# A second attention whose logits come from H times (W a), ELU moved between heads, and norms that read a sum of four chunks

## What is computed

```python
def gat_layer(x, W, a_src, a_dst, bias, src, dst, heads, out_c, concat):
    h = (x @ W).reshape(n, heads, out_c)
    al_s = jnp.einsum('nhc,hc->nh', h, a_src)      # source logit of each node
    al_d = jnp.einsum('nhc,hc->nh', h, a_dst)      # target logit of each node
    e = jax.nn.leaky_relu(al_s[src] + al_d[dst], 0.2)
    m = jax.ops.segment_max(e, dst, num_segments=n)
    ex = jnp.exp(e - m[dst])
    z = jax.ops.segment_sum(ex, dst, num_segments=n)
    alpha = ex / (z[dst] + 1e-16)
    msg = h[src] * alpha[:, :, None]
    out = jax.ops.segment_sum(msg, dst, num_segments=n)
    ...
# layer 1: second layer on elu(first layer): gat_layer(h, W2, a_src2, a_dst2, b2, ..., 1, 768, False)
```

## Time and profile before

| what | value |
|---|---|
| median of 3 runs | 3227.3 us (3222.09 to 3234.06) |
| profiled execution: its own time | 3223.88 us |
| its span, first to last instruction | 3222.1 us |
| mean granted TensorE clock | 0.970 |
| PE busy | 3017.0 us, 94% |
| DVE, ACT, POOL busy | 1723.8, 742.5, 1435.7 us |

### The profile page before, as it was taken

The page is one execution under the profiler, slowest core; times in us unless marked ns, Lnnn a source line. Parts: engine busy times, 40 slices in busy tenths (PEclk is TensorE's granted clock), DMA queues, the critical chain, the costliest instruction groups (busy, mean ns, idle before and its releaser), DMA issues.

```text
span 3222.1 us, 38156 instructions
## 1 busy us (share of the span) xinstructions
PE 3017.0 (94%) x13743; PEld 2340.4 (73%) x13753; DVE 1723.8 (53%) x2816; ACT 742.5 (23%) x1288; POOL 1435.7 (45%) x1007
## 2 busy tenths in 40 slices
PE   8999898999999996998998889899999998999988
PEld 3467576878888884776877358578888886878855
DVE  7734699575545537745785645533333336743132
ACT  1043211242223312102235221211111112212122
POOL 2022377624454442464541044456666664545610
PEclk9999999999999998998999899999999999999999
DMA  2011257311222221222210142123323332222313
GB/s 84 15 44 45 98 178 219 94 39 60 73 69 74 73 65 59 71 89 63 81 53 30 50 132 64 59 76 98 93 88 98 97 98 64 79 68 75 102 36 137
DMA packets 91282, 256.96 MB, mean 80 GB/s; under 512 B 10343, under 2 KB 10983, under 8 KB 90868
## 3 DMA queue, kind: packets, MB, share of 16 engines
q1 hardware_dynamic: 79488, 217.09, 22.1%
q10 hardware_dynamic: 11668, 38.19, 3.5%
HBM read 253.67 MB, written 1.57 MB: 79 GB/s over the span
## 4 chain that ended last, share of the span: by engine, by line
PE 84%; DVE 10%; issue 4%; ACT 2%; DMA 0%; ACTq 0%; DVEq 0%
PE ps L437 23%; PE ps L441 22%; PE ps L442 22%; PE ps L921 3%; DVE aux L2130 2%; PE ps L549 1%; PE ps L543 1%; PE ps L802 1%; PE ps L813 1%; PE ps L795 1%; PE ps L787 1%; DVE hot L2583 1%; DVE row L1938 1%; PE ps L622 1%; PE ps L1008 1%
## 5 line engine op out<-in xcount | busy, mean ns | idle before, releaser
L372 POOL TENSOR_SCALAR w_hi<-raw 128x768 fp32r<-128x768 f32 x498 | 469.3, 942 | 1607.5 <-PE ps L437 1418.3
L375 POOL TENSOR_TENSOR w_lo<-raw,w_hi 128x768 fp32r<-128x768 f32 x498 | 974.9, 1958 | 41.5
L437 PE MATMUL ps<-A_hi,w_hi 128*128 128x512 f32 x924 | 364.5, 394 | 2.2 <-DVE sel_now L2411 1.5
L441 PE MATMUL ps<-A_lo,w_hi 128*128 128x512 f32 x924 | 360.7, 390 | 0.0
L442 PE MATMUL ps<-A_hi,w_lo 128*128 128x512 f32 x924 | 360.2, 390 | 0.0
L437 PE MATMUL ps<-H_hi,w_hi 128*128 128x512 f32 x804 | 319.3, 397 | 22.3 <-issue 11.6
L441 PE MATMUL ps<-H_lo,w_hi 128*128 128x512 f32 x804 | 316.4, 394 | 0.0
L442 PE MATMUL ps<-H_hi,w_lo 128*128 128x512 f32 x804 | 315.9, 393 | 0.0
L437 PE MATMUL ps<-B_hi,w_hi 128*128 128x512 f32 x576 | 234.4, 407 | 13.6 <-DVE B_lo L1916 7.4
L441 PE MATMUL ps<-B_lo,w_hi 128*128 128x512 f32 x576 | 226.6, 393 | 0.0
L442 PE MATMUL ps<-B_hi,w_lo 128*128 128x512 f32 x576 | 226.5, 393 | 0.0
(11 more groups left out here) (510 smaller groups left out, 5632.3 us busy)
## 6 DMA issues: line engine op xcount, KB each, us to landing
raw<-stream_dram SPq DMA_DIRECT2D x552, 384.0 KB, 3.0
w_ring<-w_dram ACTq DMA_DIRECT2D x43, 384.0 KB, 3.8
u_rows<-rows_dram ACTq DMA_DIRECT2D x8, 768.0 KB, 6.0
rows<-rows_dram ACTq DMA_DIRECT2D x7, 768.0 KB, 4.0
w_last<-w_dram ACTq DMA_DIRECT2D x9, 384.0 KB, 3.6
x<-x_dram ACTq DMA_DIRECT2D x1, 1536.0 KB, 8.9
out_dram<-x ACTq DMA_DIRECT2D x1, 1536.0 KB, 5.1
orf<-orf_dram ACTq DMA_DIRECT2D x6, 192.0 KB, 3.1
```

The costliest lines, as they stand in the source:

```text
L372: pool.tensor_scalar(w_hi[:, b // 3, b % 3], raw[:, b // 3, b % 3], 1.0, 1.0, ALU.mult, ALU.mult)\
L375: pool.tensor_tensor(w_lo[:, b // 3, b % 3], raw[:, b // 3, b % 3], w_hi[:, b // 3, b % 3], ALU.subtract)\
L437: mm = pe.matmul(o, wh, xh, start=first, stop=False, skip_group_check=True)
L441: pe.matmul(o, wh, xl, start=False, stop=False, skip_group_check=True)
```

## The change

1. Layer 1's second attention. While layer 0's experts run, ScalarE loads the two attention rows and W2's six row blocks, and VectorE makes `u2` = W2 a for both rows (`out_vectors`: 12 multiply-and-sum instructions of 768 and two small ones). In `turn_n`'s first group TensorE adds, behind each chunk, three products of `u2` (2 columns) with the chunk of H: a 2x512 row of logits. VectorE copies it, TensorE turns its target part into columns and broadcasts its source part inside the second group, and `gat_rows(1)` runs in the middle of that group. `terms`, `source_row` and `gat_rows(0)` are gone. The copies of the product are made straight from PSUM, and the last two tiles' copies come behind the edge weights.
2. The ELU of chunks 0, 1 and 2 goes between the scalings of heads 4 to 7; chunks 3, 4 and 5 follow. The turned chunks use banks 4 and 5.
3. Six norms read `x[0]+x[1]+x[2]+x[3]` that VectorE has added into `scr[:, 5]` (three additions between the chunks of `gat_sum` or `add_t`), then chunks 4 and 5: three products in place of six. The additions run in every iteration of the loops `experts2` (8) and `mlp3` (4).

```diff
-            def norm(since=None):
+            def norm(since=None, summed=False):
                 use(6)
-                for j in range(KC):
+                if summed:
+                    pe.wait_ge(bank_free["dve"][4], S.seen.get(bank_free["dve"][4].name, 0) + 1)
+                    pe.matmul(ps[:, 6], ones[:, :], scr[:, 5], start=True, stop=False, skip_group_check=True)
+                for j in range(4 if summed else 0, KC):
...
+                def turned(chunks):
+                    pe.wait_ge(act_to_pe, S.due(act_to_pe))
+                    for j in chunks:
+                        b = 4 + j % 2
+                        use(b)
+                        for m in range(NT):
+                            mm = pe.transpose(ps[:, b, m * P:m * P + P], acc_n[:, m, j * P:j * P + P], ident[:, :])
+                        done(mm, b, "act")
...
+                    if h >= 5:
+                        turned(((0, 1), (2,), (3,))[h - 5])
-                unpend()
-                pe.wait_ge(act_to_pe, S.due(act_to_pe))
-                transposes(lambda m, j: acc_n[:, m, j * P:j * P + P], "act")
-                turn_n(H, "act", since=chunks_due())
-                gat_rows(0)
-                gat_rows(1)
+                turned((4,))
+                turned((5,))
+
+                def out_logits(k):
+                    if k == 0:
+                        pe.wait_ge(u2_split, 1)
+                        use(6)
+                    mm = mm3(ps[0:2, 6], u2_hi[:, k], u2_lo[:, k], H[0][:, k], H[1][:, k], k == 0, k == KC - 1)
+                    if k == KC - 1:
+                        done(mm, 6, "dve")
+
+                def out_rows(m, k):
+                    if (m, k) == (0, 2):
+                        pe.wait_ge(dve_to_pe, S.due(dve_to_pe))
+                        use(7)
+                        for n in range(NT):
+                            mm = pe.transpose(ps[:, 7, n * 2:n * 2 + 2], row[0:2, n * P:n * P + P], ident[0:2, 0:2])
+                        done(mm, 7, "dve")
+                        use(6)
+                        done(pe.matmul(ps[:, 6], ident[0:2, 0:1].to_broadcast([2, P]), row[0:2, :], start=True, stop=True), 6, "dve")
+                    if (m, k) == (1, KC - 1):
+                        pe.wait_ge(dve_to_pe, S.due(dve_to_pe))
+
+                def out_targets(g, m):
+                    if (g, m) == (1, 1):
+                        gat_rows(1)
+
+                turn_n(H, "act", mid=out_targets, since=chunks_due(), last=False, freed_by="dve", per_chunk=out_logits,
+                       inside=out_rows)
                 gat_den()
-                graph_t("dve")
+                graph_t("dve", second=True)
...
+                load_rows(ROW_L1B)
+                for k in range(KC):
+                    act.dma_start(gat_w1(k), t["w1"][GAT_W1 + KC + k]).then_inc(u2_in, 16)
...
+                gat_scaled(4)
+                elu_parts(0)
+                elu_parts(1)
+                gat_scaled(5)
+                mark(act_to_pe)
+                elu_parts(2)
+                gat_scaled(6)
+                mark(act_to_pe)
+                gat_scaled(7)
+                mark(act_to_pe)
+                for j in range(3):
+                    elu_high(j)
+                elu_parts(3)
+                elu_parts(4)
+                elu_high(3)
+                elu_parts(5)
+                elu_high(4)
+                elu_high(5)
...
+                nodes_of(0, range(NT))
+                nodes_of(1, range(2))
                 edge_weights()
+                nodes_of(1, range(2, NT))
...
+            def sum_of_x(j):
+
+                if 2 <= j < 5:
+                    S.step(dve.tensor_tensor(scr[:, 5], x[:, 0] if j == 2 else scr[:, 5], x[:, j - 1], ALU.add))
...
                 for j in range(KC):
+                    sum_of_x(j)
                     dve.wait_ge(tile_for["dve"], S.due(tile_for["dve"]))
-                    S.step(dve.tensor_tensor(scr[:, j], ps[:, j], row[:, :], ALU.mult))
+                    S.step(dve.tensor_tensor(scr[:, j % 4], ps[:, j], row[:, :], ALU.mult))
...
+            def out_vectors():
+
+                dve.wait_ge(rows_in, S.due(rows_in, 16))
+                dve.wait_ge(u2_in, KC * 16)
+                for k in range(KC):
+                    for r in range(2):
+                        ins = dve.tensor_tensor_reduce(flat[:, r * D:r * D + D], gat_w1(k), rows[:, r], 1.0, 0.0, ALU.mult, ALU.add,
+                                                       u2_all[:, k, r:r + 1])
+                    S.step(ins)
...
-                experts("experts0", 2, 10.0, True, lambda n: gat_vectors(range(3, KC)) if n == 1 else None)
+                experts("experts0", 2, 10.0, True, lambda n: gat_vectors(range(3, KC)) if n == 1 else out_vectors() if n == 3 else None)
...
+                gat_inverse(5)
+                elu_merged(0)
+                elu_merged(1)
+                gat_inverse(6)
+                elu_merged(2)
+                gat_inverse(7)
+                for j in range(3):
+                    elu_low(j)
...
+                dve.wait_ge(tile_for["dve"], S.due(tile_for["dve"]))
+                freed(dve.tensor_copy(row[0:2, :], ps[0:2, 6]), 6)
+                mark(dve_to_pe)
+                nodes_of(0, range(NT))
+                mark(dve_to_pe)
+                dve.wait_ge(tile_for["dve"], S.due(tile_for["dve"]))
+                freed(dve.tensor_copy(nv[:, 0:2, :], ps[:, 7, 0:8].rearrange("p (m r) -> p r m", r=2)), 7)
                 target_rows()
+                nodes_of(1, range(2))
                 edge_weights()
+                nodes_of(1, range(2, NT))
+                mark(dve_to_pe)
```

More of the change, by code:

```diff
@@ L485, in turn_t, with turn_n @@
                             after(3 * g + j)
-            def turn_n(X, reader, mid=None, since=None, last=True, freed_by=None):
+            def turn_n(X, reader, mid=None, since=None, last=True, freed_by=None, per_chunk=None, inside=None):
                 def tile_done(mm, b):
@@ L517, in turn_n @@
                                        k == 0, k == KC - 1)
+                            if inside:
+                                inside(m, k)
                         tile_done(mm3_, b)
@@ L521, in turn_n, with graph_t @@
                     blocks_used(3, last and g == 1)
-            def graph_t(reader, halves=False):
+            def graph_t(reader, halves=False, second=False):
                 hn = [B[h][:, :, :].rearrange("p k n -> p (k n)").rearrange("p (m d) -> p m d", m=NT) for h in range(2)]
                 for j in range(KC):
-                    if halves and j % 3 == 0:
+                    if halves and j % 3 == 0 or second and j == 3:
                         pe.wait_ge(dve_to_pe, S.due(dve_to_pe))
@@ L542, in norm @@
                         pe.wait_ge(bank_free["dve"][j], S.seen.get(bank_free["dve"][j].name, 0) + 1)
-                    mm = pe.matmul(ps[:, 6], ones[:, :], norm_src[0][:, j], start=j == 0, stop=j == KC - 1,
-                                   skip_group_check=True)
+                    mm = pe.matmul(ps[:, 6], ones[:, :], norm_src[0][:, j], start=j == 0 and not summed,
+                                   stop=j == KC - 1, skip_group_check=True)
                 done(mm, 6, "dve")
@@ L556, in norm_twice @@
             def norm_twice():
-                norm()
+                norm(summed=True)
                 return chunks_due()
@@ L1014, in part, with norm_of @@
                 return p in parts
-            def norm_of(src, since=None):
+            def norm_of(src, since=None, summed=False):
                 norm_src[0] = src
-                norm(since)
+                norm(since, summed)
             ran = lambda p: p in parts
@@ L1754, in _, with elu_parts, elu_high @@
                 mark(act_to_pe)
+                merged = [S.due(dve_to_act) for j in range(KC)]
+                def elu_parts(j):
+                    q, b = 2 * (j % 2), 4 + j % 2
+                    if j >= 2:
+                        act.wait_ge(dve_to_act, merged[j - 2])
+                    act.wait_ge(tile_for["act"], S.due(tile_for["act"]))
+                    act.activation(aux[:, q], ps[:, b], ACT.Exp, bias=col("L1_gnn_b1", j))
+                    freed(act.activation(aux[:, q + 1], ps[:, b], ACT.Relu, bias=col("L1_gnn_b1", j)), b)
+                    mark(act_to_dve)
+                def elu_high(j):
+                    act.wait_ge(dve_to_act, merged[j])
+                    act.activation(H[0][:, j], scr[:, j], ACT.Identity, bias=-1.0).then_inc(act_to_dve, 1)
                 for h in range(1, 3):
@@ L1757, in _, with nodes_of @@
                     gat_exps(h + 5)
[L1758 to L1759 removed]
                 mark(act_to_pe)
[L1761 to L1764 removed]
+                gat_scaled(3)
+                mark(act_to_pe)
[8 more added lines that the diff above has]
+                gat_scaled(7)
+                mark(act_to_pe)
+                for j in range(3):
[6 more added lines that the diff above has]
```

(17 more changed lines are left out.)

67 lines of the change are left out of this document (43 added, 24 removed).

## The result

The changed kernel takes 3197.7 us in the median of four runs (3194.0 to 3199.4), the kernel before 3228.6 beside it (3222.1 to 3234.1). The ratio is 0.9904, with a 95% interval of 0.9892 to 0.9917. That is 30.9 us less, where 32.3 were summed and 3195 was forecast. The spans of the profiled executions differ by less, 3222.1 against 3195.2 us: the profiled execution of before lies 4.8 us under its median, that of after only 0.7 us under its own.

What follows compares the result with a forecast made beforehand. TensorE, busy 94% of the span, was taken as the bound. Norms 15.4 plus gnn1's end 16.9 made 32.3 us off 3223.9, 3191.6; with 3.4 us to the median, 3195 us, range 3187 to 3209 at more than 8 in 10.

Steps and rivals of the forecast that it cites:

- Norms: Six norms each lose three chunks on TensorE, 3 x 0.857 = 2.57 us a norm, 15.4 us in all.
- The additions cost nothing: VectorE's three additions per norm, 0.65 to 2.05 us each, lie before waits for TensorE's tiles and are hidden.
- ELU and the start of turn_n: With ELU of early chunks between head scalings in gnn1, turn_n starts at 1733.5 in place of 1737.19.
- T: End of turn_n's group 0 with 18 logit products added, forecast at 1753.0 with 5.9 us at low clock.
- The rows of logits: In turn_n's second group: no wait at the row, 0.3 us before the broadcasts, last low half of edge weights at T+19.4.
- graph_t: Layer 1's graph_t starts at T+20.15 = 1773.1 in place of 1789.32, 16.2 us sooner.
- the 0.7 us extra for a full clock at its start: graph_t's first products run at full instead of low clock, saving 0.7 us more, together 16.9 us.
- Beside the experts: out_vectors' 12 products end by 1457, before TensorE needs bank 0 about 1460: no cost; at 2.4 us each, 9 us stall.
- Rival B: Middle of turn_n becomes a chain of waits and the clock falls; gnn1 gives 6 us, time 3206; chance 0.13.
- C: One of the two parts, norms or gnn1's end, gives nothing: 3210 or 3211 us; chance 0.10.
- D: Additions in the experts2 and mlp3 loops are not hidden: 2.3 us each, 83 us, 3278 us; chance 0.04.
- E: The rest, such as a stall beside the experts that eats most of the gain, no change; chance 0.03.

Runs made afterwards that it cites:

- norms_only: Kernel before with only the cheaper norms of part 3, gnn1's code left as before: 3213.9 us, ratio 0.9957 to the kernel before.
- chunk5_bank7: Changed kernel with the last ELU chunk turned into bank 7, not waiting for bank 5: 3194.6 us, 3.1 us under the changed kernel.
- gnn1_only: Changed kernel without part 3, so norms read six chunks and no sums are added: 3212.9 us, ratio 0.9948 to the kernel before.
- vectors_twice: Changed kernel with each of the 12 products of out_vectors made twice: 3218.7 us, 21 us above the changed kernel.
- both: Changed kernel with the last ELU chunk turned into bank 7 and norms reading a sum of five chunks, then chunk 5: 3192.0 us.
- sums_twice: Changed kernel with VectorE's additions in experts2 and mlp3 each preceded by a second one, 36 more: 3196.1 us, ratio 0.9893 to the kernel before.

## Why the prediction was right

The sign, the size and the reasons held: two parts that add up, each to within 1.3 us of its term.

- **Norms, 15.4 us.** Measured 14.6 by norms_only, and 7.6 to 7.9 for three norms from N to L: 2.5 to 2.6 each in the mean, where 3 x 0.857 = 2.57 was worked out. The wait for chunk 5 was to be under 0.1 us, and there is none in the six records behind gnn1. Before, six norms and one more had 84 records of `x`; after, the L554 group has 36 and the L547 group 12.
- **The additions cost nothing.** Right, and the reason as given: they lie before waits for tiles. Their size lies between the two values that were named, 1.78 us in the mean for 0.65 and 2.05, but as a mixture of 0.69 and 2.33. The Trainium skill (GPSIMD Engine Reference, section Key points) says that VectorE instructions with two SBUF inputs contend with GpSimd. The trace agrees in both directions: the additions beside a low half took 2.33 us, and the mean of GpSimd's high half went from 833 to 902 ns. GpSimd still waited 209.7 us for TensorE in that stretch, so nobody waited for its splits.
- **ELU and the start of turn_n.** Every step of ScalarE's queue came 0.4 to 0.5 us before its forecast instant (last scaling 1728.47 for 1729.0, Relu of chunk 3 done by 1732.4 for 1732.9), and so did `turn_n`: 1733.01 for 1733.5. The distance from scaling to start was forecast at 4.5 and is 4.54. The step that sets it was named too: bank 5. chunk5_bank7 takes just that away.
- **T, the end of group 0 with the logits.** 1753.0 was named; 1750.69 and three products of 0.235 make 1751.4. (The 2-column products cost what was assumed: the first three, from 1736.73 on, took 0.71 us.) The mis-sized term is the low clock: 5.9 us of it were taken over from before, and only the 3.7 us from 1733.01 to 1736.73 came. By the two prices named, 2.2 us less of low clock is 2.2 x (1 - 0.173/0.33) = 1.0 us; the start, 0.5 us early, is the rest of the 1.6.
- **The rows of logits.** Broadcasts without a wait, where 0.3 us was forecast. The edge weights' first Exp was named at T+9.6 and came at 1761.08, T+9.7. The last low half was named at T+19.4; it was done at 1769.53 + 1.46 = 1770.99, T+19.6. TensorE's one wait, 1.73 us before the sums of the last edge weights, follows from its being busy only to T+15.7, as the text had it; `graph_t` came at T+20.7 for T+20.15.
- **graph_t.** 1773.1 was named, 1772.07 measured. This was 1.0 us better. But the 0.7 us extra for a full clock at its start did not come, and this term of the sum was wrong: its first product still took 0.63 us, as in the earlier trace rows, the granted clock was 0.50 from 1771 to 1774, and from its start to the norm it took 17.80 us where the earlier trace rows have 17.52. The clock fell behind the wait of 1.73 us before the last sums. The prediction had both ends of that gap (TensorE busy to T+15.7, last low half at T+19.4) and took the clock to be full behind it all the same. The two misses nearly cancel by luck: 17.25 us to the start of `graph_t`, 16.9 forecast. gnn1_only gave 15.6 us in the medians and 17.16 from S to N.
- **Beside the experts.** `out_vectors` was to be done by 1457 and was by 1457.8; TensorE was to need bank 0 at about 1460, and vectors_twice shows 1461.45. The bound that was named, a stall of 9 us if the products ran at 2.4 us each, is the mechanism that vectors_twice ran into.
- **The two earlier norms.** S is at 1728.4 in both profiled executions, as if these norms had won nothing; the traces show where their gain is and what hides it. At the first of them after is already 3.9 us behind, before any changed line is reached. From the start of the last `x` (1268.14 before, 1272.00 after) to the centring (1272.57 and 1274.05) it is 4.43 us before and 2.05 after: 2.4 won. From this centring to the next changed norm's, before took 225.8 us, after 222.0 and norms_only 222.0, while gnn1_only with its old norms took 224.1. So the second norm won 2.1 us or more. From there to S before took 230.0 us and after 232.4. norms_only changes nothing in that stretch and has 232.8, and `both`, with every edit in it, has 230.2: so it is not the change. These two, before and `both`, are also the two of the fourteen whose granted clock was 0.97 and not 0.94 in the 60 us ahead of the target logits. That before's profile was one of the quicker runs fits its median, 4.8 us higher.

Rival B, a chain of waits inside `turn_n`, is refuted by the window at clock 1.00 and by the missing waits; what the clock does behind a short wait it had right in part, as the 1.73 us before the last sums show; C, one part without gain, by norms_only and gnn1_only. D, additions not hidden, is refuted at 36 additions in the loops and at the dose of sums_twice; the true threshold was not reached. E, a stall beside the experts, did not happen but lies only 3.0 us away.

## What to carry to other kernels

Where TensorE is full nearly everywhere, look for its few holes and for work of it that a waiting engine can do: a sum of four chunks by VectorE saved three products a norm, and logits made from H instead of H W filled a hole of 13 us. Place such work before a wait, and measure how thick the cover is: here it was 3.0 us at one place and at least a third more than was used at another, and beyond it one stall cost more than its length, because the clock fell as well. A micro-gain on TensorE just ahead of a place where VectorE is late is only a longer wait, so two small edits have to be judged by stages and not by whether their medians add up.

## What the runs showed of the hardware

- An f32 addition of 128x512 with both inputs in SBUF took 0.69 us alone and 2.33 us when it began just behind GpSimd's low half of a weight block (L379, both inputs in SBUF): in after and in sums_twice it ended 0.55 us after the low half, whatever was left of it (1.78 or 0.86 us). So its price hangs on when it starts, and doubling the count raised the load by a third. The same addition with one input in PSUM took 0.69 us beside the low half as well. GpSimd pays too: its low half took 2.16 us in sums_twice where it took 1.84 in after.
- The multiply-and-sum of 768 columns with both inputs in SBUF took 0.95 us while GpSimd was idle, and 1.57 to 2.47 us beside its low halves. A cast of only 12 columns behind them took 1.68 us and ended with the low half.
- The length of the last wait alone did not tell the clock behind it. Behind one wait of 3.68 us the products ran at a granted clock of 0.57 for 4 us; with waits of 0.90 and 0.68 us, less than half as much in all, and transposes between them, it stayed at 1.00. It stayed at 1.00 for the transposes behind the 1.92 us in the earlier trace rows, but was 0.50 for 3 us behind 1.73 us of waiting ahead of `graph_t`, and 0.54 for 7 us after 16.9 us of waiting. What decides between such cases was not tested.
